# Pair products on all 128 rows with a moving buffer of their own, and a new order of the first layer with W1's feature gathers behind tile 0's

## What is computed

```python
cont_emb = emb_table[:13][None, :, :] * conts[:, :, None]
cate_emb = emb_table[cates]
cc = jnp.concatenate([cont_emb, cate_emb], axis=1)
gram = jnp.einsum('bfd,bgd->bfg', cc, cc)
pairs = gram[:, ROWS, COLS]
X = jnp.concatenate([cont_emb.reshape(B, -1), cate_emb.reshape(B, -1), pairs], axis=1)
X = relu(layernorm(X @ W1 + b1, ln1_g, ln1_b))      # 3237 -> 1024
X = relu(layernorm(X @ W2 + b2, ln2_g, ln2_b))      # 1024 -> 1024
logit = sigmoid(X @ Wout + bout)
```

## Time and profile before

| | |
|---|---|
| time, median of 3 runs (range) | 852.54 us (851.6 to 855.34) |
| the profiled execution: its time, its span | 849.3 us, 847.5 us |
| PE matmul busy | 787.0 us (93% of the span) |
| DVE, ACT, POOL busy | 486.7, 388.5, 492.7 us |
| mean granted clock of TensorE | 0.963 of full |
| chain that ended last | PE 88%, POOL 4%, issue 3%, DVE 3%, ACT 2% |

### The profile page before, as it was taken

One profiled execution on the slowest core, in us unless ns is written; L12 is line 12 of the kernel. 1 busy time (PEld: TensorE's weight loads), 2 busy tenths in 40 slices (PEclk: granted clock), 3 DMA queues, 4 the chain that ended last, 5 costly groups with the idle time before them and its releaser, 6 DMA issues.

```text
span 847.5 us, 12350 instructions
## 1 busy us (share of the span) xinstructions
PE 787.0 (93%) x4287; PEld 638.2 (75%) x4287; DVE 486.7 (57%) x1050; ACT 388.5 (46%) x735; POOL 492.7 (58%) x458
## 2 busy tenths in 40 slices
PE   6367697999999999999999999999999999999994
PEld 1245586888888888888888888888888788888883
DVE  2444837555565555655556555565556576555666
ACT  0343736354362543625446354463538444455441
POOL 5747774776767667677677767767100143344433
PEclk9686698999999999999999999999999999999998
DMA  9973453647455473554635547364256211111000
GB/s 265 254 169 26 26 25 43 49 28 49 26 49 47 26 48 25 48 48 25 48 26 48 47 26 47 26 48 48 9 181 241 75 27 49 49 49 49 25 1 0
DMA packets 27229, 50.72 MB, mean 60 GB/s; under 512 B 11406, under 2 KB 11662, under 8 KB 27206
## 3 DMA queue, kind: packets, MB, share of 16 engines
q0 software_dynamic: 14992, 16.77, 33.2%
q1 hardware_dynamic: 9478, 24.94, 10.0%
q10 hardware_dynamic: 2736, 8.71, 2.6%
HBM read 41.99 MB, written 8.40 MB: 59 GB/s over the span
## 4 chain that ended last, share of the span: by engine, by line
PE 88%; POOL 4%; issue 3%; DVE 3%; ACT 2%; DMA 1%; ACTq 0%; DVEq 0%; POOLq 0%
PE acc L472 24%; PE acc L474 23%; PE acc L473 23%; PE tr L514 4%; PE gr L553 4%; PE tr L553 4%; POOL xb L435 3%; PE tr L497 1%; PE gr L497 1%; PE gr L648 1%; PE tr L648 1%; POOL raw_lo L421 1%; PE gr L530 1%; PE tr L523 1%; DMA xb<-in_L_rec_emb_table,idx 1%
## 5 line engine op out<-in xcount | busy, mean ns | idle before, releaser
L435 POOL DMA_INDIRECT xb<-in_L_rec_emb_table,idx x416 | 412.6, 992 | 172.3 <-issue 132.1
L472 PE MATMUL acc<-w_hi,x_hl 128*128 128x512 f32 x416 | 176.2, 424 | 7.7 <-DVE w_lo L974 7.7
L474 PE MATMUL acc<-w_hi,x_hl 128*128 128x512 f32 x416 | 165.7, 398 | 0.0
L473 PE MATMUL acc<-w_lo,x_hl 128*128 128x512 f32 x416 | 164.8, 396 | 0.0
L455 POOL TENSOR_TENSOR raw_lo<-raw_lo,raw_hi 128x1024 f32<-128x1024 f32 x15 | 35.9, 2395 | 167.3 <-ACT raw_lo L869 167.3
L718 ACT CAST xg<-x_hl 64x192 fp32r<-64x192 f32 (+1 forms) x192 | 117.2, 610 | 3.0
L472 PE MATMUL acc<-w_hi 128*128 128x512 f32 x256 | 101.0, 395 | 1.4 <-DVE raw_lo L1154 1.4
L474 PE MATMUL acc<-w_hi,w_lo 128*128 128x512 f32 x256 | 99.7, 389 | 0.0
L473 PE MATMUL acc<-w_lo,w_hi 128*128 128x512 f32 x256 | 99.7, 389 | 0.0
L472 PEld LDWEIGHTS acc<-w_hi,x_hl 128*128 128x128 f32 x416 | 79.8, 192 | 25.3 <-DVE w_lo L974 9.4
L474 PEld LDWEIGHTS acc<-w_hi,x_hl 128*128 128x128 f32 x416 | 79.4, 191 | 18.1
(11 more groups left out here) (110 smaller groups left out, 1140.2 us busy)
## 6 DMA issues: line engine op xcount, KB each, us to landing
h_scratch<-h_row ACTq DMA_DIRECT2D x16, 512.0 KB, 5.8
raw_hi<-h_scratch SPq DMA_DIRECT2D x16, 512.0 KB, 3.6
raw_lo<-in_L_rec_W SPq DMA_DIRECT2D x26, 256.0 KB, 13.5
xb<-in_L_rec_emb_table,idx POOLq DMA_INDIRECT x416, 3.6
raw_lo<-in_L_rec_W SPq DMA_DIRECT2D x8, 512.0 KB, 7.0
raw_hi<-in_L_rec_W SPq DMA_DIRECT2D x6, 512.0 KB, 6.9
raw_hi<-in_L_rec_b SPq DMA_DIRECT2D x1, 512.0 KB, 4.2
raw_hi<-in_L_rec_ln_g SPq DMA_DIRECT2D x1, 512.0 KB, 5.1
```

What stands on the lines that cost most here:

```text
L435: nc.gpsimd.indirect_dma_start(out=xb[:, f * DIM:(f + 1) * DIM], out_offset=None, in_=emb, in_offset=bass.IndirectOffsetOnAxis(ap=idx[:, p ...
L472: nc.tensor.matmul(o, a, w, start=first, stop=False)
L473: nc.tensor.matmul(o, a, v, start=False, stop=False)
L474: return nc.tensor.matmul(o, b, w, start=False, stop=last)
```

## The change

The pair products use two new buffers in place of `xg`. `g_still` [128 rows, 128 samples, 32] has hi on rows 0 to 63 and twice lo on rows 64 to 127; `g_move` [128 rows, 26 fields, 128 samples] has hi on both halves. A fill is 8 matmuls on 128 rows, whose 104 columns are now ordered field by sample, so that what `take_dots` reads lies 4 elements apart. ACT and DVE each write half of either buffer: 4 copies for a part of the fields, of twice the elements.

`sums`, `cc_rows`, `pairs` and `chosen` lose buffers of their own: the first two lie in `dots`, the last two in `h1_row`. So `take_dots` of fill 0 waits for `feat_done` and `chosen_done` of the tile before, `cate_pairs` waits for `l_trans` and for the store of the rows before, and `norm1` for `l_trans`.

The order on all engines is another. On PE, "factor" and "late" of tile x go into iteration x+1 ("factor prev", "late prev"), so does the transpose of group 1 ("own 1"), and "next 0" is the last step. In ACT's and DVE's queues norm1 of x-1 is ahead of fill 0's take, `split_group(x + 1, 1)` and `gram_copies(x + 1, 0)` are behind the splitting of the features. The last iteration has an order `LAST`. POOL gathers W1's feature rows behind all of tile 0's embeddings, in seven pieces rather than six.

```diff
--- before.py
+++ after.py
-STEADY = (0, "own 2", "own 3", 1, 13, 14, 15, "cont", 16, "gram 0", 17, 18, "gram 1", 2, "gram 2", 3, 4, 5, "gram 3",
-          6, 7, 8, 9, "next 0", "next 1", 10, "factor", 11, "late", 12)
-FIRST = (0, 1, 2, 3, 4, "own 2", 5, 6, 7, 8, "own 3", 9, 10, "cont", 11, "gram 0", "gram 1", 12, "gram 2", "gram 3",
-         "next 0", "factor", "late", "next 1")
-SECOND = (0, 1, 13, 14, 15, 16, 17, 18, 2, 3, "own 2", 4, 5, 6, "own 3", 7, 8, "cont", 9, "gram 0", "gram 1",
-          10, "gram 2", "gram 3", "next 0", "factor", 11, "late", "next 1", 12)
+STEADY = (0, 1, "factor prev", 2, "late prev", "own 1", 3, 13, 14, 15, 16, 4, 17, 5, "own 2", 18, 6, "own 3", 7, 8, "cont", 9,
+          "gram 0", 10, "gram 1", 11, "gram 2", "gram 3", 12, "next 0")
+FIRST = (0, 1, 2, 3, "own 1", 4, 5, 6, "own 2", 7, 8, 9, "own 3", 10, "cont", 11, 12, "gram 0", "gram 1", "gram 2", "gram 3",
+         "next 0")
+SECOND = (0, 1, 2, 3, "factor prev", "late prev", "own 1", 13, 14, 15, 4, 5, 6, "own 2", 16, 17, 18, 7, "own 3", 8, 9, "cont",
+          10, "gram 0", 11, "gram 1", 12, "gram 2", "gram 3", "next 0")
+LAST = (0, 1, "factor prev", 2, "late prev", "own 1", 3, 13, 14, 15, 16, "own 2", 4, 17, "own 3", 18, 5, 6, "cont", 7,
+        "gram 0", 8, "gram 1", 9, "gram 2", "gram 3", 10, 11, 12, "factor", "late")
...
-W1_BEFORE = {"own 1": (0, 1, 2), "own 2": (3, 4, 5), "own 3": (6, 7, 8, 9, 10), "dots 0": (11,), "dots 2": (12,),
-             "choose": (13, 14, 15, 16), "end": (17, 18)}
+W1_BEFORE = {"own 1": (0, 1, 2, 3), "own 2": (4, 5, 6), "own 3": (7, 8, 9), "copies": (10,), "dots": (11, 12),
+             "own 1 next": (13, 14, 15), "end": (16, 17, 18)}
...
-        xg = sb("xg", [P, 2, STEPS, SAMPLES, QUAD], F32R)
+        g_still = sb("g_still", [P, P, QUAD], F32R)
+        g_move = sb("g_move", [P, CATE, P], F32R)
         x_hl = sb("x_hl", [P, 2, EK, P], F32R)
-        f_slots = sb("f_slots", [P, 2, FK, P], F32R)
+        f_slots = sb("f_slots", [P, 2, NF, P], F32R)
...
         dots = sb("dots", [P, CATE, QUAD])
-        pairs = sb("pairs", [P, CATE, QUAD])
-        sums = sb("sums", [P, CATE * CATE])
-        chosen = sb("chosen", [P, DIAGS * DIAG])
+        sums = dots[:, :, :].rearrange("p g b -> p (g b)")[:, 0:CATE * CATE]
+        cc_rows = dots[:, EK:CATE, :]
         feats = sb("feats", [P, PACKED])
-        cc_rows = sb("cc_rows", [P, EK, QUAD])
         h1_row = sb("h1_row", [P, HID])
+        pairs = h1_row[:, 0:CATE * QUAD].rearrange("p (g b) -> p g b", b=QUAD)
+        chosen = h1_row[:, 0:DIAGS * DIAG]
         conts_sb = sb("conts_sb", [P, TILES * CONT])
...
-            return banks.rearrange("p u (c s g) -> p s u c g", c=PER_FILL, s=SAMPLES)[:, s]
+            return banks.rearrange("p u (c g s) -> p s u c g", c=PER_FILL, s=SAMPLES)[:, s]
...
-        def x_part(h, n, of, to):
+        def still_part(h, n, of):
 
             a, b = X_PARTS[n]
-            return x_hl[DIM * of:DIM * (of + 1), h, a:b, DIM * to:DIM * (to + 1)].rearrange("p k b -> p b k")
-
-        def xg_part(h, n, of, to):
+            return (g_still[DIM * h:DIM * (h + 1), :, EK * of + a:EK * of + b],
+                    x_hl[DIM * of:DIM * (of + 1), h, a:b, :].rearrange("p k b -> p b k"))
+
+        def move_part(n, of, to):
 
             a, b = X_PARTS[n]
-            rows = xg[DIM * to:DIM * (to + 1), h, :, :, :].rearrange("p j s f -> p (j s) f")
-            return rows[:, :, EK * of + a:EK * of + b]
+            return (g_move[DIM * to:DIM * (to + 1), EK * of + a:EK * of + b, :],
+                    x_hl[DIM * of:DIM * (of + 1), 0, a:b, :])
...
-                nc.gpsimd.indirect_dma_start(
-                    out=raw_lo[EK + s][0:m, :], out_offset=None, in_=W1,
-                    in_offset=bass.IndirectOffsetOnAxis(ap=rows_sb[0:m, s:s + 1], axis=0),
-                ).then_inc(w1_in[EK + s], 16)
+                pieces = ((0, m, s, w1_in[EK + s]),) if s != FT else ((0, V_AT, s, w1_in[EK + s]), (PART, m, NF, w1_tail))
+                for a, b, column, landed in pieces:
+                    nc.gpsimd.indirect_dma_start(
+                        out=raw_lo[EK + s][a:b, :], out_offset=None, in_=W1,
+                        in_offset=bass.IndirectOffsetOnAxis(ap=rows_sb[0:b - a, column:column + 1], axis=0),
+                    ).then_inc(landed, 16)
...
             pool.wait_ge(rows_in, 16)
             gather(0, 0, first=True)
+            for s in range(NF):
+                feature_rows_of(s)
             gather(1, 1)
             with pool.Fori(0, (TILES - 2) // 2) as i:
                 for u in range(2):
...
-                    j = PER_FILL * q + c
-                    for h in range(2):
-                        for u in range(2):
-                            at_u = slice(DIM * u, DIM * (u + 1))
-                            to = (gr, tr)[q % 2][:, u, c * SAMPLES * CATE:(c + 1) * SAMPLES * CATE]
-                            last = nc.tensor.matmul(to, xg[at_u, 0, j, :, :].rearrange("p s f -> p (s f)"),
-                                                    xg[at_u, h, j, :, 0:CATE], start=h == 0, stop=h == 1)
+                    for u in range(2):
+                        j = SAMPLES * (STEPS * u + PER_FILL * q + c)
+                        to = (gr, tr)[q % 2][:, u, c * SAMPLES * CATE:(c + 1) * SAMPLES * CATE]
+                        last = nc.tensor.matmul(to, g_still[:, j:j + SAMPLES, :].rearrange("p s f -> p (s f)"),
+                                                g_move[:, :, j:j + SAMPLES], start=True, stop=True)
                 last.then_inc(gram_ready, 1)
 
...
             pe.wait_ge(setup_done, 1)
-            for g in range(2):
-                transpose_group(0, g, first=True)
+            transpose_group(0, 0, first=True)
...
-                    for to in range(2):
-                        last = nc.scalar.copy(xg_part(0, n, of, to), x_part(0, n, of, to))
+                    nc.scalar.copy(*still_part(0, n, of))
+                for of in range(2):
+                    last = nc.scalar.copy(*move_part(n, of, 0))
                 last.then_inc(xg_hi, 1)
 
...
                 act.wait_ge(gram_ready, FILLS * x + q + 1)
-                if q == 0 and not first:
-                    act.wait_ge(pairs_done, x)
+                if q == 0:
+                    act.wait_ge(feat_done, x + 1)
+                    if not first:
+                        act.wait_ge(chosen_done, x)
                 for s in range(2):
                     last = nc.scalar.mul(dots_part(q, s), gram_part(q, s), 0.5)
...
                 act.wait_ge(ln, LN_STEPS * x + 8)
+                act.wait_ge(l_trans, x + 1)
                 if not isinstance(x, int) or x >= 1:
                     act.wait_ge(h1_out, 16 * x)
                 nc.scalar.activation(h1_row[:, 0:HALF], acc[par][:, 0, :], ACT.Identity,
...
                 if k < EK:
                     act.wait_ge(w1_up[k], 16)
-                if k == EK:
-                    act.wait_ge(v_done, 1)
                 if k == EK + FT:
+                    act.wait_ge(w1_tail, 16)
                     act.wait_ge(b1_in, 16)
-                    nc.scalar.copy(raw_lo[k][V_AT:V_AT + CONT, :],
-                                   acc[1][0:CONT, :, :].rearrange("p h n -> p (h n)")).then_inc(v_in, 1)
                     act.wait_ge(v_in, 1)
                 m = rows_of(k)
                 nc.scalar.copy(w1_hi[0:m, k, :], raw_lo[k][0:m, :]).then_inc(w1_rounded, 1)
...
+            act.wait_ge(v_done, 1)
+            nc.scalar.copy(raw_lo[EK + FT][V_AT:V_AT + CONT, :],
+                           acc[1][0:CONT, :, :].rearrange("p h n -> p (h n)")).then_inc(v_in, 1)
             split_group(0, 0)
             w1_before("own 1")
             split_group(0, 1)
@@ -800,35 +813,32 @@
                 split_group(x, 2)
                 if first:
                     w1_before("own 3")
+                gram_copies(x, 1)
                 split_group(x, 3)
-                gram_copies(x, 1)
+                if first:
+                    w1_before("copies")
                 gram_copies(x, 2)
+                if first:
+                    w1_before("dots")
+                else:
+                    norm1(x - 1, 1 - par)
+                    h1_store(x - 1)
                 for q in range(FILLS):
-                    if first and q in (0, 2):
-                        w1_before(("dots 0", "dots 2")[q // 2])
-                    if q == 2 and not first:
-                        norm1(x - 1, 1 - par)
-                        h1_store(x - 1)
                     take_dots(x, q, first)
-                if first:
-                    split_group(x + 1, 0)
-                    factor_hi(x)
-                    w1_before("choose")
-                    choose_pairs(x)
-                    late_features_hi(x)
-                    tail_features_hi(x)
-                    split_group(x + 1, 1)
-                    w1_before("end")
-                    gram_copies(x + 1, 0)
-                    return
```

(65 more changed lines are left out.)

28 lines of the change are left out of this document (16 added, 12 removed).

## The result

| | before | after |
|---|---|---|
| time, median of 4 runs each (range) | 852.07 us (851.55 to 855.34) | 923.73 us (923.57 to 924.92) |
| ratio, 95% interval | | 1.084 (1.082 to 1.086) |
| profiled execution: time, span | 849.3, 847.5 us | 923.8, 922.0 us |
| PE busy, mean granted clock | 787.0 us, 0.963 | 800.8 us, 0.920 |

The account below looks back on a forecast made before the run. PE bound the kernel before, at 35.57 us an iteration; afterwards a take-to-split chain would. Start 125 + 13 x 39.3 + end 246 = 882 us of span, put as 885 us, 4% slower; range 858 to 904.

Parts of the forecast that it names:

- What PE would wait for: At each next tile's first K tile, PE stands 4.2 us for the group 0 split queued behind ACT's choice.
- Rival D: In steady iterations PE still sets the pace, 33.5 us each, 805 us in all; chance 0.03.
- Rivals C and E: Start against iterations: C, start gains more, tile 2 at 108, 840 us, chance 0.04; E, they cancel, 851, chance 0.05.
- The fills: Pair products on PE: a fill falls from 1.03 to 0.52 us, four saving 2.06 us an iteration.
- The takes: DVE's reads of the pair products, now stepping over 4 elements: still 1.10 us each, no extra cost.
- rival B: Each iteration 1.0 to 1.7 us longer by slower stepped takes or undiminished pair-product cost, about 902 us; chance 0.13.
- The store: Transpose of the pairs waits for the rows' store from `h1_row`, landing 33.0 us after the first K tile.
- The clock: After PE's wait in each iteration, work at half pace loses 1.5 us, bounds 0 and 1.7.
- Rival A: The chain binds each iteration but PE's clock stays up, 13 x 1.5 us less, 865 us; chance 0.15.
- The copies: ACT's and DVE's copies for pair products: ACT 11.4 us a tile against 7.4, DVE 6.5 to 8.2 against 4.6.
- The start: With W1's gathers behind tile 0's, tile 1 starts at 80 us and tile 2 at 125, bounds 115 and 132.
- The range: Whole kernel: 858 to 904 us should hold 8 in 10, around a forecast of 885.

Follow-up runs that it names:

- e3: Changed kernel with the next tile's group 0 split ahead of choice and pairs on ACT and DVE: 859.66 us, ratio 1.009 to the kernel before.
- f7: Changed kernel with the old pair products of the kernel before: 929.28 us, ratio 1.091 to the kernel before.
- e4: Changed kernel with 16 unused 512-column matmuls on PE in the wait behind "next 0": 896.66 us, ratio 1.053 to the kernel before.
- e1: Changed kernel with the tail's gather of K tile 16's slab taking 80 rows, not 79: 911.28 us, ratio 1.070 to the kernel before.
- e2: Changed kernel with the pair products' moving operand read as one run of 104 numbers: 921.60 us, ratio 1.082 to the kernel before.
- g1: Kernel before with new pair products and W1's gathers behind tile 0's, of 128 rows where the slab has them: 842.51 us, ratio 0.991.
- f8: Changed kernel with norm1 and next split earlier, W1 pieces of 128, 32 and 80 rows, K tile 12 last: 853.72 us, ratio 1.002 to the kernel before.

## Why the prediction was right or wrong

**What PE would wait for** was right: the mechanism, its place (ACT's split behind its choice) and its length, 4.03 us against 4.2. The way from the start of the transpose of the pairs to the next first K tile is 4.62 us (423.61 to 428.23), forecast 4.8. Rival D needed PE to stay full, and e3 shows how near it was: one exchange of two entries leaves 1.4 us of wait. Rivals C and E needed tile 2 at 108 or 115; it came at 142.65.

**The fills** were a term mis-sized: 0.83 us, not 0.52. I had chosen the end of the range at which everything is saved, though the rows left it open. It counts because the path to the takes was another than I had written. I had the takes bound by norm1 and the features (ready at 28.3), and PE's fill 3 "not late". Without the clock's loss of 2.2, the features are ready 27.8 us after the first K tile, near to the forecast, and the first take waits for them; but the take of fill 1 then waits 0.49 us for PE and that of fill 2 1.15. So the last take ends at 33.9, where I had 32.7: of the 1.2 us, the three fills up to fill 2, at 0.31 more each, are 0.9, and the rest was not taken apart. The takes themselves, with their stepped read, came as forecast (1.07 to 1.14 us against 1.10), so rival B's first half fell and its second half was half true.

**The store** was put as the bound of the transpose, at 33.0; it landed in time and bound nothing (the transpose starts 0.18 us after the last take). This error of mine was hidden by the one above.

**The clock** was mis-sized: after a wait of 4.03 us it stays at 0.50 for 4.4 us of work (from 428.23 until the pace doubles), so 2.2 us are lost, not 1.5. I took the 3.1 us of the one case before; f7 shows that one case could not tell, since behind equal waits it lasted from 2.7 to over 4.8 us. Run e4 prices it at 1.9 by taking it away. Rival A falls. The transpose starts at 34.1 without the clock's loss, where I had the store's 33.0: 1.1. With the clock's 0.7, less 0.2 for the shorter way behind it, that is the 1.6 us that each iteration lies over the forecast, 20.4 in thirteen.

**The copies** were near: ACT's two kinds take 99.9 + 62.9 us in sixteen tiles, 10.2 a tile, forecast 11.4. No wait of PE in the steady part is put down to them.

**The start** is the step that failed most plainly: a queue that I costed at nothing. I wrote that W1's gathers go out quickly behind tile 0's, and costed what stands behind them on POOL at nothing. The first part held: K 0 at 28.14, K 4 at 45.37 and fill 0 at 70.93, against 28, 44.5 and 70. But these gathers now stand in one block directly ahead of tile 1's in POOL's queue, and I looked only at when tile 0's get out. The diff's own line had the 79 rows. Run e1 gives 12.4 of the 14.3 us by which tile 1 was late back, and tile 2 is then at 129.16, inside the bounds of 115 and 132 that I had set. What is left, 4.2 us at tile 2, lies in tile 0's takes and iteration 1's fills and clock, and was not taken apart.

**The range** was too narrow, and not for the start alone: with the gather mended (e1) the time is 911.28 us, still over its end of 904. The iteration of 40.87 us lay inside my bounds of 37.3 and 41, but the range had left out their upper end. The start had bounds for every cost that I had listed, and none for a queue that I had not. Both errors went the same way.

## What to carry to other kernels

When an instruction is moved within a queue, write down what is queued behind it at its new place as well as what is freed at the old one; and for a DMA, look at its number of rows, since one of 79 rows held the queue for 17 us where with 80 it stood 4.2 us at most. When an engine falls idle once in each iteration, first look whether what it waits for is queued behind something that nobody needs yet: here exchanging two entries in the queues was worth 64 us, the cheaper matmuls 5.5. A wait of 1.4 us in each iteration did not lower the clock here and one of 4 us did, so the cut from the one to the other paid 4.7 us an iteration where the wait itself fell by 2.6. And when the engine that sets the pace is relieved, count the next one's work by the distance of its starts: POOL looked busy for 25.6 of 35.57 us, and the cheaper pair products ran into it.

## What the runs showed of the hardware that I had not expected

- Matmuls of 104 columns on all 128 rows, each with a new stationary operand, follow each other at 104 ns, with the moving operand in one run or in runs of four (e2); on alternating halves of 64 rows they follow at 64 ns. Twice the rows at one time gained a fifth, not half. With 512 columns a load on the same 128 rows lay inside the matmul before it, at 0.22 us from start to start.
- With a gather of 79 rows of 4 KB in flight, the DMA share fell to 0.06 at 27 GB/s, and POOL's queue was held for 17 us; with 80 rows the longest such hold was 4.2 us (e1), and where K tiles 17 and 18 were gathered with 128 rows as well (g1, f8) there was none among W1's gathers.
- Behind waits of the same length, 4.03 us, PE's clock stayed at 0.50 for 2.7 us in one tile and over 4.8 in another (f7).
- A gather of POOL is busy for 0.94 us, but in no trace here does the next start sooner than 1.24 us after it: 26 of them fill at least 32 us of an iteration.
- Sixteen useless matmuls in a 4 us wait made the kernel 27 us faster, as the clock stayed up behind them.
- On one chip the kernel before took 1169.8 us, at a mean granted clock of 0.84 in place of 0.96; there the changed order with the old pair products was faster than the kernel before (ratio 0.938). Why that chip grants less, and why the order then wins, stays open.
